# First attention of a fused decoder: the score banks' start values written by ScalarE and VectorE instead of matmuls, and another order of the subtraction and the value products

## The reference, cut to what matters

```
q = rope(x @ Wq + bq); k = rope(x @ Wk + bk); v = x @ Wv + bv
scores = q . k * D ** -0.5                       # masked to -inf where k > q or q - k >= 64
combined = concat([scores, sinks], -1)           # one more column per head
probs = softmax(combined)[..., :-1]
out = (probs . v) @ Wo + bo
```

## Time and profile before

| | us |
|---|---|
| median of 3 runs | 1679.07 |
| lowest and highest run | 1675.69, 1680.11 |
| the profiled execution's own time | 1674.48 |
| its span, first to last instruction | 1672.7 |
| TensorE busy in the span | 1604.6 (96%) |
| VectorE busy | 989.6 (59%) |
| ScalarE busy | 730.5 (44%) |
| GpSimd busy | 508.7 (30%) |
| mean granted TensorE clock, share of full | 0.992 |

### The profile page before, as it was taken

How to read it: one execution, slowest core, us unless ns; L and a number is a source line. 1 busy time by engine, 2 the same in 40 slices (tenths; PEclk the granted TensorE clock), 3 DMA queues, 4 the chain that set the end, 5 groups by cost and what they waited for, 6 DMA issues and landing times.

```text
span 1672.7 us, 24191 instructions
## 1 busy us (share of the span) xinstructions
PE 1604.6 (96%) x9704; PEld 1332.0 (80%) x9704; DVE 989.6 (59%) x1659; ACT 730.5 (44%) x1222; POOL 508.7 (30%) x335
## 2 busy tenths in 40 slices
PE   7999999999899999989999989999889999999998
PEld 7997667778688888867889987787668888888887
DVE  6555663455667675487758748244767455554554
ACT  2113664322577765666621146432635344353442
POOL 3875542620100002332118634111512432222321
PEclk9999999999899999999999999999999999999999
DMA  4110003133312004410001110111001111111111
GB/s 164 51 64 27 2 2 129 40 109 121 107 51 64 14 1 161 157 38 1 1 0 63 51 39 1 37 51 32 21 1 57 51 51 57 51 45 51 51 57 45
DMA packets 28579, 88.51 MB, mean 53 GB/s; under 512 B 4154, under 2 KB 4282, under 8 KB 28215
## 3 DMA queue, kind: packets, MB, share of 16 engines
q1 hardware_dynamic: 28468, 86.96, 15.5%
HBM read 85.11 MB, written 1.84 MB: 52 GB/s over the span
## 4 chain that ended last, share of the span: by engine, by line
PE 85%; DVE 8%; ACT 5%; issue 1%; POOL 0%; ACTq 0%; DVEq 0%
PE PS L255 17%; PE PS L257 17%; PE PS L256 17%; PE PS L260 6%; PE PS L1040 5%; PE PS L1058 4%; PE PS L1390 3%; PE PS L946 3%; PE PS L1405 2%; PE PS L555 2%; PE PS L579 1%; PE PS L1637 1%; PE PS L1625 1%; PE PS L545 1%; DVE sm L1659 1%
## 5 line engine op out<-in xcount | busy, mean ns | idle before, releaser
L301 POOL TENSOR_TENSOR HL<-stg,HL 128x1024 fp32r<-128x1024 f32 (+2 forms) x111 | 244.6, 2207 | 825.1 <-ACT HL L296 807.1
L255 PE MATMUL PS<-XT,HL 128*128 128x448 f32 x608 | 224.4, 369 | 4.3 <-DVE XT L336 3.7
L256 PE MATMUL PS<-XT,HL 128*128 128x448 f32 x608 | 222.6, 366 | 0.0
L257 PE MATMUL PS<-XT,HL 128*128 128x448 f32 x608 | 222.5, 366 | 0.0
L296 ACT ACTIVATE HL<-stg 128x1024 fp32r<-128x1024 f32 (+2 forms) x111 | 104.2, 944 | 216.0 <-PE PS L257 199.5
L255 PE MATMUL PS<-HL,XT 128*128 128x512 f32 (+1 forms) x380 | 137.5, 362 | 2.2 <-DVE XT L1909 1.4
L257 PE MATMUL PS<-HL,XT 128*128 128x512 f32 (+1 forms) x380 | 134.9, 355 | 0.0
L256 PE MATMUL PS<-HL,XT 128*128 128x512 f32 (+1 forms) x380 | 134.7, 355 | 0.0
L255 PEld LDWEIGHTS PS<-XT,HL 128*128 128x128 f32 x608 | 114.6, 188 | 16.5 <-DVE XT L336 4.9
L256 PEld LDWEIGHTS PS<-XT,HL 128*128 128x128 f32 x608 | 114.7, 189 | 9.1
L257 PEld LDWEIGHTS PS<-XT,HL 128*128 128x128 f32 x608 | 114.6, 188 | 9.2
(11 more groups left out here) (288 smaller groups left out, 3611.9 us busy)
## 6 DMA issues: line engine op xcount, KB each, us to landing
stg<-in_wst SPq DMA_DIRECT2D x87, 512.0 KB, 3.7
stg<-in_wst SPq DMA_DIRECT2D x16, 352.0 KB, 3.3
stg<-in_wst SPq DMA_DIRECT2D x16, 320.0 KB, 3.5
wsum<-in_wfc SPq DMA_DIRECT2D x8, 512.0 KB, 3.9
wsum<-in_wpj SPq DMA_DIRECT2D x8, 512.0 KB, 3.5
raw<-in_wfc SPq DMA_DIRECT2D x8, 512.0 KB, 7.9
stg<-in_wst SPq DMA_DIRECT2D x16, 256.0 KB, 2.8
raw<-in_wpj SPq DMA_DIRECT2D x7, 512.0 KB, 7.0
```

The costliest lines, as they stand in the source:

```text
L255: e.matmul(out, lh, rh, start=start, stop=False)
L256: e.matmul(out, lh, rl, start=False, stop=False)
L257: return e.matmul(out, ll, rh, start=False, stop=stop)
L301: e.tensor_tensor(slot(k)[:, 1, 0:n], stg[k % NSTG][:, 0:n], slot(k)[:, 0, 0:n].bitcast(F), A.subtract).then_inc(*done("pool_w", k))
```

## The change

Four things change, all in the first attention:

1. The 12 matmuls per step that write mask and sinks are gone. Instead a new `fill(u)` copies the mask to the 896 score columns of a unit's two banks and the sinks to its 16 sink columns, two instructions. VectorE does it for even units, behind its two `largest` and before `value0_out` and `sums(2w)`; ScalarE for odd units, behind `power(2w+1)`. Each waits for the exponential of the unit that was in the banks before. `scores(w)` waits for both fills and begins with the products.
2. Ahead of the loop TensorE writes each of the four banks once (`clear`, four matmuls of 456 columns). VectorE's `fill(0)` waits for the second of them and stands in its queue behind `value0_out(5)`; ScalarE's `fill(1)` waits for the fourth.
3. TensorE's order in a step becomes `scores(w)`, `turn(2w-3)`, `less(2w)`, `values(2w-4)`, `less(2w+1)`, `turn(2w-2)`, `values(2w-3)`.
4. `ones`, `skh`, `skl` and `maskR` of this stage are not made any more. The wait of ScalarE for the last transpose of the layer norm ahead of `one` is gone.

ScalarE's order of `turned`, `out` and `power` is the same as before.

```diff
-            e.tensor_copy(ones[:, :], C("ones")[:, 0:S]).then_inc(*done("dve_p0", "ones"))
...
-            e.tensor_copy(skh[:, :], M("sinks", S)).then_inc(*done("dve_p0", "skh"))
...
-            e.tensor_tensor(skl[:, :], M("sinks", S), skh[:, :].bitcast(F), A.subtract).then_inc(*done("dve_p0", "sinks"))
...
+        def sinks_of(u):
+            i = 2 * (u % 2)
+            sk = M("sinks", S).rearrange("p (s h i) -> p s i h", s=2, h=4)[:, u // 2 % 2, i:i + 2, :]
+            return sk.unsqueeze(3).to_broadcast([S, 2, 4, 2])
+
+        def mask_of():
+            return C("mask0", S).unsqueeze(1).unsqueeze(1).to_broadcast([S, 2, 4, S])
+
+        def whole0(u):
+            i = 2 * (u % 2)
+            return PS[0:S, i:i + 2, 0:4 * S + 8].rearrange("p i (h k) -> p i h k", h=4)
...
             def scores(w):
                 b, s = w // 2, w % 2
-                for i in range(4):
-                    e.wait_ge(*(upon("act_a0", "exp", 2 * w - 2 + i // 2) if w else upon("dve_p0", 16 + i // 2, i % 2)))
-                    e.matmul(bank0(i)[:, :, 0:S], one[0:S, 0:S], maskR[:, :].unsqueeze(1).to_broadcast([S, 4, S]), start=True,
-                             stop=True)
-                for part in (skh, skl):
-                    for i in range(4):
-                        e.matmul(bank0(i)[:, :, S:S + 2], ones[32 * i:32 * i + 1, :], sinks_of(part, w, i), start=False, stop=True,
-                                 skip_group_check=True)
+                e.wait_ge(*upon("dve_a0", "fill", 2 * w))
+                e.wait_ge(*upon("act_a0", "fill", 2 * w + 1))
...
-            e.wait_ge(*upon("act_a0", "mask"))
-            e.wait_ge(*upon("dve_p0", "sinks"))
+            e.wait_ge(*upon("act_a0", "one"))
+            for i in range(4):
+                e.wait_ge(*upon("dve_p0", 16 + i // 2, i % 2))
+                e.matmul(bank0(i), one[0:S, 0:S], one[0:S, 0:S + 2].unsqueeze(1).to_broadcast([S, 4, S + 2]), start=True,
+                         stop=True).then_inc(*done("pe_a0", "clear", i))
...
                 if w > 1:
                     turn(2 * w - 3)
+                if w < W0:
+                    less(2 * w)
+                if w > 1:
                     values(2 * w - 4)
                 if w < W0:
-                    less(2 * w)
+                    less(2 * w + 1)
                 if 0 < w <= W0:
                     turn(2 * w - 2)
-                if w < W0:
-                    less(2 * w + 1)
...
         def act_att0(e):
+            def fill(u):
+                if u > 1:
+                    e.wait_ge(*upon("act_a0", "exp", u - 2))
+                e.activation(whole0(u)[..., 0:S], mask_of(), ACT.Copy)
+                e.activation(whole0(u)[..., S:S + 2], sinks_of(u), ACT.Copy).then_inc(*done("act_a0", "fill", u))
+
+            e.activation(one[:, :], C("ident"), ACT.Copy).then_inc(*done("act_a0", "one"))
+            e.wait_ge(*upon("dve_p0", "sinks"))
+            e.wait_ge(*upon("pe_a0", "clear", 3))
+            fill(1)
...
                 if w < W0:
                     power(2 * w + 1)
+                if w < W0 - 1:
+                    fill(2 * w + 3)
                 if 0 < w <= W0:
                     turned(2 * w - 2)
...
         def dve_att0(e):
+            def fill(u):
+                if u:
+                    e.wait_ge(*upon("act_a0", "exp", u - 2))
+                e.tensor_copy(whole0(u)[..., 0:S], mask_of())
+                e.tensor_copy(whole0(u)[..., S:S + 2], sinks_of(u)).then_inc(*done("dve_a0", "fill", u))
+
+            e.wait_ge(*upon("pe_a0", "clear", 1))
+            fill(0)
             for w in range(W0 + 1):
...
                     largest(2 * w)
                     largest(2 * w + 1)
+                    if w < W0 - 1:
+                        fill(2 * w + 2)
```

More of the change, by code:

```diff
@@ L141, in build @@
         one = misc("one", [128, 128], R)
-        ones = misc("ones", [128, S], R)
-        skh = misc("skh", [S, 32], R)
-        skl = misc("skl", [S, 32], R)
         nm = misc("nm", [S, 4, 2])
@@ L473, in dve_proj0 @@
             rope0(e, 3)
-            e.tensor_scalar(M("sinks", S), M("sinks", S), 8.0, None, A.mult).then_inc(*done("dve_p0", "sinks8"))
-            e.tensor_copy(ones[:, :], C("ones")[:, 0:S]).then_inc(*done("dve_p0", "ones"))
-            e.wait_ge(*upon("dve_p0", "sinks8"))
-            e.tensor_copy(skh[:, :], M("sinks", S)).then_inc(*done("dve_p0", "skh"))
-            e.wait_ge(*upon("dve_p0", "skh"))
-            e.tensor_tensor(skl[:, :], M("sinks", S), skh[:, :].bitcast(F), A.subtract).then_inc(*done("dve_p0", "sinks"))
+            e.tensor_scalar(M("sinks", S), M("sinks", S), 8.0, None, A.mult).then_inc(*done("dve_p0", "sinks"))
             for u in range(4, 20):
@@ L520, in build @@
         U0, W0, U1 = 32, 16, 16
-        def sinks_of(part, w, i):
-            row = part[32 * i:32 * i + 1, :].rearrange("p (s h i) -> p s i h", s=2, h=4)[:, w % 2, i, :]
-            return row.unsqueeze(2).to_broadcast([1, 4, 2])
+        def sinks_of(u):
[7 more added lines that the diff above has]
+            return PS[0:S, i:i + 2, 0:4 * S + 8].rearrange("p i (h k) -> p i h k", h=4)
         def keys(ap, h=4):
@@ L631, in out @@
                 e.activation(QO[:, u // 2, g:g + 4, :], psv(6 + u % 2), ACT.Copy).then_inc(*done("act_a0", "o", u))
-            e.wait_ge(*upon("pe_ln", "x", NT - 1))
-            e.activation(one[:, :], C("ident"), ACT.Copy)
-            e.activation(maskR[:, :], C("mask0", S), ACT.Copy).then_inc(*done("act_a0", "mask"))
+            def fill(u):
[7 more added lines that the diff above has]
+            fill(1)
             for w in range(W0 + 2):
```

## The result

The changed kernel takes 1692.38 us (median of 4 runs, 1689.13 to 1693.88), the kernel before 1677.38 (4 runs): ratio 1.0096, 95% interval 1.0078 to 1.0115. That is 13 to 19 us slower (0.8 to 1.2%), 15.0 by the medians. 1689.5 was forecast, in 1683 to 1697.

The account below looks back on a forecast made before the run. TensorE bound the 7.40 us step before; after the change ScalarE's chain would. Start 1.0, step 0 0.3, VectorE's V copy 0.3, steps 2 and 3 2.1, steps 4 to 14 6.05, end 0.4: +10.2, forecast 1689.5 us, range 1683 to 1697.

Parts of the forecast that it names:

- The deciding point: ScalarE's queue: the copy-out, waiting for delayed values, stands ahead of the even exponential, which starts 5.05 us into the step.
- The ordinary step: Steps 4 to 14 of the first attention: 7.95 us instead of 7.40, +6.05 us over eleven steps.
- from the subtraction to the values: TensorE: the values start 0.47 us after the even subtraction starts, at 3.59 into the step.
- the small fill: ScalarE's copy of the 16 sink columns into the odd unit's banks: 0.23 us, between bounds of 0.21 and 0.29.
- The writes to PSUM: Mask copies of 896 columns into the score banks: 0.95 us taken for ScalarE, 1.1 for VectorE.
- VectorE hidden: VectorE's fill of the even unit delays nothing: 0.33 us to spare per step, unless it costs over 1.4.
- Start, steps 2 and 3, end: Clears and first fills +1.0 us; rounding between exponentials in steps 2 and 3 +2.1; later odd exponential in last step +0.4.
- Step 0: First step of the loop: 8.18 us instead of 7.84, +0.3.
- step 1: Second step of the loop: its 8.23 us stays within 0.1, so 0 added.
- the clock as a rival: TensorE, 79% busy, loses clock: 1.7 us per fall, 1705 us with falls in most steps; chance 0.04.
- VectorE as the bound: VectorE's fill into PSUM takes 1.33 us or more and sets the step; at 1.7, 1694 us; chance 0.12.
- TensorE as the bound: TensorE's work still sets the step, 6.65 us, so the kernel is faster, 1670.5 us; chance 0.04.

Follow-up runs that it names:

- experiment 1: Changed kernel with ScalarE's copy-out moved behind the even exponential: 1679.16 us, ratio to the kernel before 1.0024.
- experiment 3: Kernel before with only TensorE's new order, masks and sinks still by matmuls: 1688.18 us, ratio 1.0065.
- experiment 6: Changed kernel with VectorE copying the mask twice in each of its fills: 1703.49 us in one run.
- experiment 2: Changed kernel with TensorE's order put back as before, fills kept: 1686.59 us, ratio to the kernel before 1.0061.
- experiment 7: Changed kernel with TensorE doing values(2w-4) first, then both subtractions, fills kept: 1681.61 us, ratio to the kernel before 1.0036.
- experiment 4: Kernel before with VectorE filling the even unit's banks from step 1 on, matmuls still writing the odd unit's: 1674.05 us, ratio 0.9988.
- experiment 5: Changed kernel with blanks, unused matmuls into a free bank at each step's end to keep TensorE busy: 1686.32 us, ratio to the kernel before 1.006.
- experiment 8: Kernel before with VectorE filling the even unit's banks, matmuls the odd one's, both subtractions together behind values(2w-4): 1670.69 us, ratio 0.9973.

## Why the prediction was right, and where it was short

- **The deciding point held.** ScalarE's unchanged order lets the copy-out, which waits for values moved behind the subtraction, hold the even exponential. Forecast 5.05 into the step, measured 5.16; experiment 1 shows it is this that costs 0.63 per step.
- **The ordinary step** was forecast at 7.95, measured 8.06. Three terms differ: from the subtraction to the values 0.57, not 0.47 (I took the gap from a subtraction to a transpose; values behind a subtraction start 0.57 later in experiments 1, 3 and 6 too, and no run shows why); from ScalarE's last end to the first scores 0.11, not 0.04; and the small fill 0.17, not 0.23. Over 11 steps that is +7.3 instead of +6.05.
- **The writes to PSUM**, unseen before, came near the values I took: ScalarE 0.92 (0.95 taken), VectorE 1.09 (1.1 taken), 0.17 for 16 columns on either. The Trainium skill's rule ("ScalarE: Activation LUTs", step-by-step section) that ScalarE writes PSUM faster than SBUF agrees in sign: 0.92 here against 0.95 for 896 elements from SBUF to SBUF, though that instruction writes 128 partitions and rounds, so the memory is not the only difference.
- **VectorE hidden:** 0.33 forecast to spare; 0.33 idle ahead of its maxima in the changed kernel, 0.45 to spare by experiment 6.
- **Start, steps 2 and 3, end:** +1.15 (1.0), together +2.5 (2.1 and 0.3 for VectorE in step 2), +0.5 (0.4). Step 0: 8.12 (8.18).
- **The step that failed is step 1**, "the 8.23 stays within 0.1". It took 9.77. Its work would: with blanks it took 8.27. But TensorE is now idle for 2.59 us ahead of step 1 and for 2.13 ahead of step 4, and the clock fell in both. I had the clock as a rival with 0.04 of chance, at 1.7 for one fall and 15 or more for falls in most steps, and asked whether ordinary steps with 79% busy would lose it. They did not; the first steps, with longer idle, did, twice in the profiled execution, for 1.5 and 1.0 us. So forecast and that rival came true together, and treating them as exclusive made the sum short by 2.5 us.
- On that rival the Trainium skill's rule ("TensorE: Matmul & The Clock Gate", PE-mode transpose) said that transposes don't count as busy: ordinary steps with 16 transposes, a gap of 1.2 us and one of 0.35 kept clock 1.00, so nothing here shows it.
- The rivals with VectorE as the bound and with TensorE as the bound are refuted for the changed kernel by experiments 1 and 6, and the one with TensorE by its idle of 1.18 us ahead of the scores, too.

The forecast sum was +10.2. The stage cost +14.3: the difference is 2.5 from the two falls, 1.2 from the ordinary steps, and small terms. That the total came within 2.9 us (1692.38 for 1689.5) is in part luck: the forecast stood on a median of 1679.07 for the kernel before, which is 1677.38 with one more run. The rise itself was forecast at 10.4 from that median and measured at 15.0.

## What to carry to other kernels

Before an operation is moved forward in one engine's queue, read the queues of the engines that wait for what it is moved past: here the exponential could not use an earlier subtraction, since ScalarE had the copy-out of the delayed values in front of it. Work that is taken from a busy engine and given to an engine on the return path of a buffer that is reused saved nothing here (ScalarE's fill with its waits takes 1.18 us, the matmuls took 1.19); given to an engine with idle at that point (VectorE for the even unit), it saved 0.18 us per step, and 0.41 together with an order in which nothing stands between the two subtractions. Look also at the first, unfilled steps of a pipeline: what is covered later is bare there.

## What the runs showed of the hardware that was not expected

- In the changed kernel an idle of TensorE of 2.59 us was followed, 1.2 us after TensorE had begun again, by 3.4 us at half the clock, in work that was then continuous. In the changed kernel and in experiments 1, 2, 6 and 7, each with fills by ScalarE and no blanks, the first five steps have two to four such stretches; in the kernel before and in experiments 3, 4, 5 and 8 there is none in the stage. In the changed kernel a gap of 1.2 us and one of 0.35 in each of ten ordinary steps brought none; in experiment 6, with gaps of 1.55 and 0.66, two of ten ordinary steps had one (9.73 and 9.65 us instead of 8.74).
- Neither the length of one idle nor the 1.2 us behind it foretells a fall. In the changed kernel the gaps of 1.83 and 2.12 us ahead of steps 2 and 3 brought none, and in experiment 6 the longest of all, 2.96 us, brought none, as these windows show:

```profile
148.58:151.54 2.96, 0.00 (x1) 0.00 (x0) 2.32 (x4) 2.41 (x4) 0.00 (x0) 1.00 0.00 0
151.54:154.00 2.46, 2.46 (x70) 2.35 (x71) 2.42 (x4) 0.00 (x0) 0.60 (x1) 1.00 0.03 7
154.00:158.00 4.00, 3.96 (x33) 3.58 (x31) 2.64 (x5) 1.15 (x2) 2.72 (x2) 1.00 0.00 0
```

  In experiment 1, behind the same idle of 2.59 us, the clock is at 0.50 as soon as TensorE is back at 145.87:

```profile
145.87 3.35 PE L549 MATMUL PS<-Kt,QO 32*112 32x112 f32 x64 [2.59 <-ACT PS L635]
...
146.00:147.00 1.00, 1.00 (x24) 1.00 (x28) 0.97 (x3) 0.00 (x0) 0.04 (x1) 0.50 0.00 0
```

- A fill of 16 sink columns costs 0.17 us on either engine, less than the 0.21 of the shortest instruction of ScalarE in the earlier trace rows.
- With identical code the stretch behind the stage takes from 1404.2 to 1410.5 us in ten traces, the longer the more of it is at the lower clock.
